# Chunk 0's output projection moved into the last four attention blocks, and three program blocks joined into one

## What is computed

```python
mod = silu(cond) @ Wada + bada
sh_a, sc_a, gt_a, sh_m, sc_m, gt_m = split(mod, 6, axis=1)
xm = layernorm(x, g1, be1) * (1 + sc_a) + sh_a
q, k, v = split_heads(xm @ Wqkv)
x = x + gt_a * (causal_attention(q, k, v) @ Wproj + bproj)
xm = layernorm(x, g2, be2) * (1 + sc_m) + sh_m
x = x + gt_m * (gelu(xm @ W1 + b1) @ W2 + b2)
```

## Time and profile before

| | us |
|---|---|
| three runs | 2222.29, 2209.69, 2208.9 |
| median | 2209.69 |
| profiled execution, its own time | 2210.89 |
| its span, first to last instruction | 2209.1 |
| busy in the span: PE / DVE / POOL / ACT | 2146.1 / 1286.2 / 957.7 / 926.8 |
| mean granted TensorE clock | 0.990 of full |

### The profile page before, as it was taken

The page is one execution under the profiler, slowest core; times in us unless marked ns, Lnnn a source line. Parts: engine busy times, 40 slices in busy tenths (PEclk is TensorE's granted clock), DMA queues, the critical chain, the costliest instruction groups (busy, mean ns, idle before and its releaser), DMA issues. The chain is left out here.

```text
span 2209.1 us, 30720 instructions
## 1 busy us (share of the span) xinstructions
PE 2146.1 (97%) x11326; PEld 1444.3 (65%) x11326; DVE 1286.2 (58%) x2872; ACT 926.8 (42%) x1780; POOL 957.7 (43%) x380
## 2 busy tenths in 40 slices
PE   6999999999999999999999999899999999999999
PEld 5888885454445545445544544677888888888887
DVE  4777876777777777777777753795312222122122
ACT  2111115555566655656566565435322222222222
POOL 2001007969889796997979782770000000000000
PEclk9999999999999999999999999999999999999999
DMA  6538347235252433625234323595211011011010
GB/s 229 209 134 295 129 153 177 49 75 120 69 130 53 105 71 74 140 64 120 64 86 94 74 82 97 178 323 176 72 53 58 1 58 58 1 57 36 22 39 20
DMA packets 129309, 223.28 MB, mean 101 GB/s; under 512 B 8574, under 2 KB 26054, under 8 KB 128968
## 3 DMA queue, kind: packets, MB, share of 16 engines
q1 hardware_dynamic: 108568, 180.43, 30.1%
q10 hardware_dynamic: 20592, 40.90, 5.0%
HBM read 146.31 MB, written 74.98 MB: 100 GB/s over the span
## 5 line engine op out<-in xcount | busy, mean ns | idle before, releaser
L1190 ACT ACTIVATE prob<-st 128x512 f32<-128x512 f32 (+3 forms) x1280 | 604.6, 542 | 398.5 <-PE st L1366 382.9
L1161 POOL TENSOR_TENSOR psum_k<-psum_k,prob 128x2048 f32<-128x2048 f32 (+1 forms) x150 | 662.9, 4419 | 20.1 <-ACT prob L1190 4.9
L1247 DVE TENSOR_REDUCE part<-mx 128x1 f32<-128x512 f32 x707 | 462.2, 685 | 106.5 <-PE mx L1346 104.0
L1366 PE MATMUL st<-q_st,k_st 98*128 98x512 f32 (+3 forms) x1280 | 487.5, 391 | 3.7 <-PE r_ps L1390 1.4
L1346 PE MATMUL mx<-k_st,qx_st 96*128 96x512 f32 (+3 forms) x1196 | 467.7, 405 | 18.9 <-DVE part L1243 5.4
L1777 DVE TENSOR_TENSOR m_g_lo<-m_g,m_g_hi 128x512 fp32r<-128x512 f32 x128 | 88.6, 692 | 477.2 <-ACT m_g_hi L1692 477.0
L1366 PEld LDWEIGHTS st<-q_st,k_st 98*128 98x128 f32 x1280 | 242.1, 190 | 187.7 <-issue 104.6
L1346 PEld LDWEIGHTS mx<-k_st,qx_st 96*128 96x128 f32 x1196 | 225.7, 190 | 167.4 <-DVE part L1247 96.6
L1243 DVE CUSTOM_DVE_ANT_0 unused<-mx,mask_row 128x512 bf16<-128x512 f32 (+2 forms) x489 | 232.8, 485 | 111.5 <-PE mx L1346 107.5
L1685 ACT ACTIVATE m_g<-m_hid,vcol 128x512 f32<-128x512 f32 x128 | 88.2, 689 | 469.0 <-PE m_hid L1876 469.0
L1383 PE MATMUL o_ps<-prob,v_sb 128*32 128x512 f32 (+3 forms) x2560 | 284.2, 550 | 0.6 <-POOL prob L1144 0.6
(11 more groups left out here) (172 smaller groups left out, 2587.0 us busy)
## 6 DMA issues: line engine op xcount, KB each, us to landing
k_st<-qk_scratch SPq DMA_DIRECT2D x96, 256.0 KB, 8.1
qx_st<-qk_scratch SPq DMA_DIRECT2D x96, 256.0 KB, 4.9
q_st<-qk_scratch SPq DMA_DIRECT2D x96, 256.0 KB
...
```

The costliest lines, as they stand in the source:

```text
L1161: nc.gpsimd.tensor_tensor(dst, src, prob[:, s % BUF, :, m:], ALU.add).then_inc(pool_added, 1)
L1190: nc.scalar.activation(prob[:, s % BUF, h, m:], st[n % RING][:, m:], ACT.Exp, scale=SCALE).then_inc(exp_done, 1)
L1247: nc.vector.tensor_reduce(most, bank[:, 0:w], AX.X, ALU.max).then_inc(mx_free, 1)
L1366: nc.tensor.matmul(st[n % RING][:, m:], k_st[u][0:MROWS, h, kt * P:(kt + 1) * P], q_st[0:MROWS, pos % 2, h, m:], start=True, stop=True).th ...
```

## The change

`phase_project_mlp` returns its five engine programs like the other two stages, and all three run in one program block: the barrier is gone, and semaphores order what the barrier did.

Chunk 0's 48 projection matmuls go into blocks 17 to 20 of the last group, 12 each, one token tile of 128 a block, into the `mx` banks; DVE adds their residual there and, once, bias to x. In blocks 17 to 19 they stand in fours of three between the scores, in block 20 ahead of the products. For that the last group's items end at block 13 (`LAST`) with the final turn in block 14; the weights are gated in blocks 3 and 4 and split in blocks 4 to 6; the bias in block 7; SP loads chunk 0's o once the weights are gated, its x after the last maxima, chunk 1's o as before, and chunk 1's x and chunk 2's o after the last scores. ACT makes chunk 0's `o_hi` in block 13, POOL its `o_lo` at steps 28 to 31; chunk 1's `o_hi` and `o_lo` are made where chunk 0's were. The accumulator banks `p_acc` 1 to 3 swap places so that the last bank in use comes last. The diff's core:

```diff
-                  ("o_hi0", [P, KT, CH], F32R), ("o_lo0", [P, KT, CH], F32R), ("p_raw", [P, KT, D], F32))
-        self.p_hi, self.p_lo, self.o_hi, self.o_lo, self.p_raw = at[0:4:2], at[1:4:2], at[4], at[5], at[6]
-        at = over(*((n, [P, KT, D], F32) for n in ("under_p_hi0", "p_full0", "under_p_hi1", "p_full1", "under_o_hi0", "o_in0", "x0", "o_in1")))
-        self.p_full, self.o_in, self.x0 = at[1:4:2], [at[5], at[7]], at[6]
+                  *((n, [P, KT, CH], F32R) for n in ("o_hi0", "under_x0", "o_lo0", "o_lo1", "o_hi1", "o_lo2", "o_hi2")))
+        self.p_hi, self.p_lo = at[0:4:2], at[1:4:2]
+        self.o_hi, self.o_lo = [at[4], at[8], at[10]], [at[6], at[7], at[9]]
+        at = over(*((n, [P, KT, D], F32) for n in ("under_p_hi0", "p_full0", "under_p_hi1", "p_full1", "under_o_hi0", "x0", "o_in0",
+                                                   "o_in1", "under_o_hi1", "o_in2", "under_o_hi2", "x1")))
+        self.p_full, self.o_in, self.xs_c = at[1:4:2], [at[6], at[7], at[9]], [at[5], at[11]]
+        _, self.p_raw = over(("under_p_raw", [P, 6, KT, D], F32), ("p_raw", [P, KT, D], F32))
...
-        LATER, LAST, HELD = 3, 15, 8
+        LATER, LAST, HELD, PROJECT = 3, 13, 8, 17
...
-        rest = [it for it in self.items[len(self.tail):self.items.index(QC - 1) + 1]
+        rest = [it for it in self.items[len(self.tail):self.items.index(QC - 1)]
...
+            if b == LAST + 1:
+                found = [QC - 1]
+            if 0 <= b - PROJECT < TT:
+                found = found + [("project", b - PROJECT)]
...
-    PREPARE = L.own_until() + 1
+    PREPARE, FIRST_HIGH, FIRST_LOW = 3, 13, 28
...
+                if not more:
+                    sp.wait_ge(p_ready, BATCH)
+                    load_o(0)
...
-                    sp.dma_start(E.o_in[0][:, :, :], K.o[0:KT, :, 0:CH].rearrange("g p n -> p g n")).then_inc(o_loaded, 16)
+                    load_x(0, K.x0_loaded)
...
-                    sp.wait_ge(p_ready, BATCH)
-                    sp.dma_start(E.x0[:, :, :], x[0:CH, :].rearrange("(t p) d -> p t d", p=P)).then_inc(K.x0_loaded, 16)
                     steps_done(g, 2)
-                    sp.dma_start(E.o_in[1][:, :, :], K.o[0:KT, :, CH:2 * CH].rearrange("g p n -> p g n")).then_inc(K.o1_loaded, 16)
+                    load_o(1)
                 store_o(g, 2)
                 stored_o(g, 2)
                 if not more:
+                    steps_done(g, QC - 1)
+                    load_x(1, K.x1_loaded)
+                    load_o(2)
...
+                    if not more and 0 <= s - FIRST_LOW < KT:
+                        o_low(0, s - FIRST_LOW)
                 if not more:
                     for t in range(KT):
-                        pool.wait_ge(o_hi_ready, t + 1)
-                        nc.gpsimd.tensor_tensor(E.o_lo[:, t, :], E.o_in[0][:, t, :], raw(E.o_hi[:, t, :]), ALU.subtract).then_inc(o_lo_ready, 1)
+                        o_low(1, t)
...
+                if n == 0:
+                    act.wait_ge(mx_ready, ready_count(NG - 1, L.through(2, False), False))
...
-                    if not more and PREPARE <= b - 1 < PREPARE + BATCH:
+                    if not more and 0 <= b - 1 - PREPARE < BATCH:
                         weights_high(b - 1 - PREPARE)
-                    if not more and b - 1 == PREPARE + BATCH:
-                        first_o_high()
+                    if not more and b in (FIRST_HIGH, L.NB):
+                        o_high(0 if b == FIRST_HIGH else 1)
...
+            def with_bias():
+
+                dve.wait_ge(K.x0_loaded, 16)
+                dve.wait_ge(gbias_ready, 1)
+                for s in range(TT):
+                    nc.vector.tensor_tensor(E.xs_c[0][:, s, :], K.gbias[:, 0, :], E.xs_c[0][:, s, :], ALU.add).then_inc(K.xb_ready, 1)
+
+            def residual(ready, s, bank):
+
+                dve.wait_ge(mx_ready, ready + 1)
+                dve.wait_ge(K.xb_ready, s + 1)
+                nc.vector.tensor_tensor(E.xs_c[0][:, s, :], bank[:, :], E.xs_c[0][:, s, :], ALU.add).then_inc(K.x2_ready, 1)
+                dve.wait_ge(K.x2_ready, s + 1)
+                dve.sem_inc(mx_free, 1)
...
+                    if not more and L.projected(b) and L.projected(b)[0] == 0:
+                        with_bias()
...
-                    if not more and b == PREPARE:
-                        gate_weights()
+                    if not more and 0 <= b - PREPARE < BATCH:
+                        gate_weights(b - PREPARE)
+                    if not more and b - PREPARE == 2 * BATCH:
+                        gate_bias()
...
-                    dve.wait_ge(o_lo_ready, KT)
...
+            def project(g, s, i, t):
+
+                out, cols = mx[i % RING], slice(s * P, (s + 1) * P)
+                if s == t == 0:
+                    pe.wait_ge(p_hi_ready, 2)
+                    pe.wait_ge(p_split, 1)
+                    pe.wait_ge(o_hi_ready, KT)
+                    pe.wait_ge(o_lo_ready, KT)
+                if t == 0:
+                    pe.wait_ge(mx_free, item_count(g, i))
+                for k, (a, c) in enumerate(terms(E.o_hi[0][:, t, cols], E.o_lo[0][:, t, cols], E.p_hi[0][:, t, :], E.p_lo[0][:, t, :])):
+                    ins = nc.tensor.matmul(out[:, :], a, c, start=(t == 0 and k == 0), stop=(t == KT - 1 and k == 2))
+                if t == KT - 1:
+                    ins.then_inc(mx_ready, 1)
...
+                    share = None if more else L.projected(b)
+                    if share and b == L.NB:
+                        for t in range(KT):
+                            project(g, *share, t)
...
+                            if share and h % 2 == 0:
+                                project(g, *share, 2 * e + h // 2)
...
+        acc = acc[:1] + [acc[1 + (LATEST - k) % 3] for k in (2, 1, 0)]
...
-        block = ctx.enter_context(nc.Block())
...
-            sp.wait_ge(acc_ready, TT)
+            sp.wait_ge(x2_ready, TT)
...
-            low(1)
...
-            high(1)
...
-            dve.wait_ge(K.x0_loaded, 16)
-            for t in range(TT):
-                nc.vector.tensor_tensor(xs[0][:, t, :], K.gbias[:, 0, :], xs[0][:, t, :], ALU.add).then_inc(xb_ready, 1)
-            residual(0)
...
-                if n:
+                if n > 1:
                     pe.wait_ge(x2_ready, TT * (n - 1) + s + 1)
+                elif s:
+                    pe.wait_ge(E.item_taken, L.NI * (NG - 1) + LATEST + s)
                 cols = slice(s * P, (s + 1) * P)
                 b = batch(n)
                 for t in range(KT):
-                    if n and s == 0:
-                        pe.wait_ge(lo_ready, KT * (n - 1) + t + 1)
+                    if s == 0:
+                        if n == 1:
+                            pe.wait_ge(K.o_lo_ready, KT + t + 1)
+                        else:
+                            pe.wait_ge(lo_ready, KT * (n - 2) + t + 1)
...
-            for n in range(2):
-                for s in range(TT):
-                    project(n, s)
+            for s in range(TT):
+                project(1, s)
...
-            block = early.enter_context(nc.Block())
...
+        project = phase_project_mlp(nc, K, E, L, x, w1, w2, b2, out)
+        block = ctx.enter_context(nc.Block())
+
+        @block.sync
+        def _(sp):
+            qkv.sync(sp)
+            attention.sync(sp)
+            project.sync(sp)
```

More of the change, by code:

```diff
@@ L87, in __init__ @@
         self.x0_loaded = ctx.enter_context(nc.semaphore("b_x0_loaded"))
-        self.o1_loaded = ctx.enter_context(nc.semaphore("b_o1_loaded"))
+        self.x1_loaded = ctx.enter_context(nc.semaphore("b_x1_loaded"))
+        self.o_loaded = [ctx.enter_context(nc.semaphore(f"b_o_loaded{n}")) for n in range(3)]
+        self.o_hi_ready = ctx.enter_context(nc.semaphore("b_o_hi_ready"))
+        self.o_lo_ready = ctx.enter_context(nc.semaphore("b_o_lo_ready"))
+        self.xb_ready = ctx.enter_context(nc.semaphore("b_x_with_bias_ready"))
+        self.x2_ready = ctx.enter_context(nc.semaphore("b_x2_ready"))
         with ExitStack() as staged:
@@ L261, in norm, with project, projected @@
         return not isinstance(it, int) and it[0] == "norm"
+    def project(self, it):
+        return not isinstance(it, int) and it[0] == "project"
+    def projected(self, b):
+        return next(((it[1], i) for it, i in ((self.tail[i], i) for _, i in self.tail_at[b]) if self.project(it)), None)
     def diagonal(self, s):
@@ L284, in queue @@
         return self.items if more else self.tail
-    def own_until(self):
-        return max(b for b, found in self.tail_at.items() for _, i in found if not self.norm(self.tail[i]))
     def group(self, g, it):
@@ L956, in phase_attention @@
         gbias_ready = sem("b_gbias_ready")
[L957 to L959 removed]
+        o_loaded, o_hi_ready, o_lo_ready = K.o_loaded, K.o_hi_ready, K.o_lo_ready
+        E.item_taken, E.o_copied, E.r_taken = mx_free, o_copied, r_taken
         held = sem("b_wait_carrier")
@@ L1235, in item @@
```

(74 more changed lines are left out.)

53 lines of the change are left out of this document (28 added, 25 removed).

## The result

| | before | after |
|---|---|---|
| median of the comparison's runs, us | 2208.90 (11 runs) | 2223.88 (11 runs) |
| profiled execution, its own time | 2210.89 | 2230.34 |
| its span | 2209.1 | 2228.4 |

The two medians are 15.0 us apart (0.7%); the ratio on record is 1.0074, 95% interval 1.0047 to 1.0101: the change costs about 16 us (10 to 22). Forecast were 2218 with a range of 2195 to 2230; the time lies in the range and 6 us above the point, and within 1% of the kernel before, as the larger part of the chances said. Of the change itself only half was forecast, 8.6 us.

A forecast was written before the change was run, and what follows sets the result against it. POOL was taken to bound blocks 1 to 8, and DVE, DMA and PE in turn the chunk loop. Terms 0.3 - 0.9 + 20 + 4.7 - 13.5 - 2 = +8.6 on 2210.9 gave 2219.5, 2218 for the runs' median; range 2195 to 2230.

The forecast's parts named there:

- Closer maxima, +0.3: Last head group: items of blocks 2 to 15 packed into 2 to 13, mostly hidden in PE's waits; +0.3 us.
- Blocks 14 to 16, -0.9: Last group: these blocks lose items and a 0.99 us PE wait, block 16's slow clock staying (0); -0.9 us.
- Weights on DVE beside the additions, +20: Blocks 3 to 7: DVE's weight instructions wait for POOL's long additions and stop PE; +20 us, bounds 0 and 33.5.
- The walk's single steps: Instruction-by-instruction delays from DVE meeting POOL: block 4 +10.6, block 5 +7.8, block 7 +2.6; sum 21.0 us.
- second rival: PE's clock drops after stops in blocks 4 and 5 and in emptier blocks: 12.1 us more, 2230; chance 0.10.
- second way to the +20: Blocks 3 to 7: 33.5 us of DVE work and waits against 12 to 13 us free leaves 20.5.
- Projection, +4.7: Blocks 17 to 20: 10.9 us of matmuls, 5.0 hidden, 1.2 regained by the clock; +4.7 us, bounds 3 and 10.9.
- Behind the attention, -13.5: Last attention matmul to chunk 1's statistics: 30.1 us shrinks to 16.6; -13.5 us.
- 1.25 of Newton steps: Behind the attention: DVE's steps between chunk 0's root and its norm take 1.25 us.
- The loop, -2: Chunk loop: loads of chunks 1 to 3 lead the norm by some 5 us more; -2 us, bounds 0 and -10.6.
- The DMA piece: Chunk loop: a 10.58 us transfer in the chain at 1460.17, taken as the most the loop could gain.
- third rival: The loop behind the norm is transfer-bound: 10.6 us instead of 2 comes back, 2210, no change; chance 0.15.

The follow-up runs named there:

- number 1: Changed kernel with the weights gated in blocks 9 and 10, split in 11 and 12, bias in 13; 2208.75 us, ratio 1.0016 to the kernel before.
- number 2: Kernel before with only the early weight work added (gating in blocks 3 and 4, splits 5 and 6, bias 7); 2227.87 us, ratio 1.0085.
- number 3: Changed kernel with each batch's gating in one DVE instruction instead of four, same early blocks; 2209.73 us, ratio 1.0001 to the kernel before.
- numbers 6: Changed kernel with one gating instruction per batch, weight steps moved to blocks 9 to 15, ACT's root ahead of chunk 2's `o_hi`; 2203.44 us, ratio 0.9979.
- Number 8: The kernel of numbers 6 with POOL held until chunk 0's norm is done before chunk 2's `o_lo`; 2205.26 us, ratio 0.9982.

## Why the prediction was right or wrong

**Closer maxima, +0.3:** right. Blocks without weight instructions last as before (block 8 5.96, block 12 6.20). Block 7's 0.2 belongs here too: it lasts 5.03 in number 1 as well, where no weights are near.

**Blocks 14 to 16, -0.9:** right. The slow-clock stretch moved from block 16 to block 15 (8.93 at 0.81) and stayed one, as "0" for it said.

**Weights on DVE beside the additions, +20:** right in mechanism and sum (+21.2), and shown: number 1 takes it away, number 2 makes it in the old kernel, number 3 makes it small by fewer meetings. The rule of the Trainium skill ("SBUF — State Buffer", "Who interferes with whom") that a DVE instruction with two SBUF inputs is blocked entirely by a GpSimd one that reads SBUF, when it comes second, holds here within 0.15 us: the split of 6.33 us in number 1 is 4.2 of addition and 2.15 of its own, 2.29 when alone. The walk's single steps were less right than their sum. It had 10.6 + 7.8 + 2.6 of waiting; the waits were 9.9 and 6.3, and the third did not occur, since the second split found POOL idle. In their place came the clock: 4.6 us in blocks 4 and 5, from halved stretches of 10.2 us each, of which 4.0 and 6.6 us lay behind the waits. That is the second rival's mechanism at the point of about 5 us that it named, inside the forecast's sum: two errors that cancel, and that part of the match is luck. The prediction's second way to the +20, by DVE's free time, misread it: the windows of blocks 3 to 7 before leave DVE 14.8 us, not 12 to 13, and that would have made 18.7 instead of 20.5.

**Projection, +4.7:** mis-sized, +6.0. Block 17 +1.6, block 18 -0.3 (its clock came back to full), blocks 19 and 20 +4.7. The 5.0 us taken as hidden in waits for exponentials plus 1.2 of clock were 4.9 in all, the clock's share included.

**Behind the attention, -13.5:** mis-sized, -11.1. The new wait for the root behind chunk 2's `o_hi` was where and about what was said (3.21 for 3.2), but that match is luck again: the forecast's own times, T + 9.6 and T + 6.2, make 3.4, and both came later, the variance at T + 7.2 because its last step met POOL (1.09 instead of 0.17), the root at T + 10.3. The step that failed is "1.25 of Newton steps (1411.99 less 1407.62 and the 3.1)": they took 3.2 (1428.40 to 1431.61), 2.0 more. They met POOL's `o_lo` of chunk 2, which now runs in the same microseconds. It is the same rule as for the gating, applied in blocks 3 to 7 and not carried to steps of 128x4; numbers 6 and 8 show it. The root's delay of 0.7 is that of its load, 8.5 us instead of 7.7; the bias and the residual took 0.3 less than forecast.

**The loop, -2:** nothing. The DMA piece stayed (9.65 for 10.58), but it was no measure of the loop: PE was idle there for only 6.1 us in all, so 10.6 could never come back, and the third rival falls with it. PE's idle time did shrink, by 1.0. What the forecast left out is the clock: PE waits 2.5 us for chunk 1's norm, 1.5 before, and two halved stretches lie in the loop, 5.6 us together, where before there was none. By half of that, 2.8 us is an estimate of what they cost at most; it would cover the missing 2.2. No run tried it. Number 8 says that an earlier start is given on in part; what takes the remainder there, DVE against POOL again or the loads of `o_in`, was read from one trace and stays open.

So of the 7.7 us between the forecast sum and the measured one without the 3.0, 2.4 lie behind the attention, 2.2 in the loop, 1.3 in the projection, 1.2 in the stops and 0.6 elsewhere. The four large ones missed to the same side: each gain was taken at what its own chain allows, without the neighbours that it newly meets and the clock that its waits cost.
